# Attention of a macaron block: half slots of two key blocks replaced by groups of three, with one exponential a block

## The reference

```python
x = x + 0.5 * ffn(layernorm(x))
x = x + attn(layernorm(x))
x = x + 0.5 * ffn(layernorm(x))

def attn(x, WQ, WK, WV, WO):
    Q, K, V = (einsum('bsd,hkd->bhsk', x, W) for W in (WQ, WK, WV))
    scores = einsum('bhqd,bhkd->bhqk', Q, K) / sqrt(16)
    scores = where(tril(ones((4096, 4096))), scores, -inf)
    attn = einsum('bhqk,bhkv->bhqv', softmax(scores), V)
    return einsum('bhsv,hdv->bsd', attn, WO)
```

## Time and profile before

| | us |
|---|---|
| median of three runs | 1996.3 (1994.75 to 1996.97) |
| span of the profiled execution | 1995.0 |
| before attention's slots | 373.9 |
| attention with all three steps, 373.9 to 1728.8 | 1354.9 |
| the last 23 slots, without maxima | 51.9 |
| output projection and second feed-forward layer | 214.3 |

### The profile page before, as it was taken

The page is one execution under the profiler, slowest core; times in us unless marked ns, Lnnn a source line. Parts: engine busy times, 40 slices in busy tenths (PEclk is TensorE's granted clock), DMA queues, the critical chain, the costliest instruction groups (busy, mean ns, idle before and its releaser), DMA issues.

```text
span 1995.0 us, 58983 instructions
## 1 busy us (share of the span) xinstructions
PE 1949.6 (98%) x24312; PEld 1198.9 (60%) x24312; DVE 1677.5 (84%) x3630; ACT 1355.3 (68%) x1626; POOL 304.6 (15%) x736
## 2 busy tenths in 40 slices
PE   5999999999999999999999999999999999999999
PEld 3777776555555555555555555555555555569998
DVE  7655566699999999999999999999999999847663
ACT  5312221588888888888888888888888888884444
POOL 2100000011101111111110111111111101134444
PEclk9999999899999999999999999999999999999999
DMA  6111221212111111211111111111122111101110
GB/s 196 51 51 51 74 77 51 74 40 52 40 47 46 44 42 39 53 40 49 45 44 39 44 48 41 50 43 44 41 46 46 39 53 29 60 28 64 59 48 22
DMA packets 82812, 102.20 MB, mean 51 GB/s; under 512 B 16752, under 2 KB 45168, under 8 KB 82544
## 3 DMA queue, kind: packets, MB, share of 16 engines
q1 hardware_dynamic: 81920, 98.03, 17.4%
q10 hardware_dynamic: 624, 0.40, 0.1%
HBM read 68.46 MB, written 29.36 MB: 49 GB/s over the span
## 4 chain that ended last, share of the span: by engine, by line
PE 92%; DVE 4%; ACT 2%; issue 1%; DMA 1%; POOL 0%; SPq 0%; POOLq 0%; ACTq 0%; DVEq 0%
PE PS L1142 33%; PE PS L1269 32%; PE PS L1119 7%; PE PS L1089 6%; PE PS L1249 6%; PE PS L1328 4%; PE PS L1194 2%; PE PS L1113 1%; PE PS L1055 1%; ACT PG L700 1%; DVE BNS L745 1%; DVE OA L798 1%; DMA PG<-w_exp_t 1%; ACT OA L608 1%; POOL QT L577 0%
## 5 line engine op out<-in xcount | busy, mean ns | idle before, releaser
L700 ACT ACTIVATE PG<-PS 128x1024 f32<-128x1024 f32 (+1 forms) x1152 | 1116.0, 977 | 233.8 <-PE PS L1249 173.2
L930 DVE TENSOR_REDUCE MXP<-PS 128x1 f32<-128x512 f32 x1792 | 1099.7, 685 | 20.5 <-PE PS L1142 20.4
L1249 PE MATMUL PS<-QT,KT 50*128 50x512 f32 (+1 forms) x2304 | 802.3, 434 | 0.0
L1142 PE MATMUL PS<-KT,QT 48*128 48x512 f32 (+3 forms) x2304 | 797.1, 431 | 2.6 <-DVE MXP L930 2.3
L1269 PE MATMUL PS<-PG,VH 128*17 128x128 f32 x16896 | 727.5, 276 | 0.4 <-ACT PG L700 0.3
L1269 PEld LDWEIGHTS PS<-PG,VH 128*17 128x17 f32 x16896 | 400.5, 97 | 412.4 <-issue 363.4
L1142 PEld LDWEIGHTS PS<-KT,QT 48*128 48x128 f32 x2304 | 340.2, 185 | 251.8 <-issue 141.9
L1249 PEld LDWEIGHTS PS<-QT,KT 50*128 50x128 f32 x2304 | 335.1, 185 | 10.3 <-issue 9.9
L926 DVE CUSTOM_DVE_ANT_0 PS<-PS,MASK 128x128 f32<-128x128 f32 (+3 forms) x512 | 249.2, 506 | 72.7 <-PE PS L1142 66.9
L557 POOL TENSOR_SCALAR_AFFINE_SELECT PG<-PG 128x128 f32<-128x128 f32 x512 | 136.3, 292 | 995.8 <-ACT PG L700 995.0
L626 ACT ACTIVATE PG<-PS,GB 128x512 f32<-128x512 f32 x128 | 90.3, 706 | 171.3 <-PE PS L1089 171.3
(11 more groups left out here) (110 smaller groups left out, 1197.2 us busy)
## 6 DMA issues: line engine op xcount, KB each, us to landing
QT<-q_parts SPq DMA_DIRECT2D x256, 64.0 KB
KT<-k_parts SPq DMA_DIRECT2D x256, 64.0 KB
q_parts<-OA SPq DMA_DIRECT2D x16, 512.0 KB, 2.8
QT<-q_parts SPq DMA_DIRECT2D x256, 32.0 KB
k_parts<-OA SPq DMA_DIRECT2D x16, 512.0 KB, 4.6
KT<-k_parts SPq DMA_DIRECT2D x256, 32.0 KB
o_parts<-OS SPq DMA_DIRECT2D x128, 64.0 KB
OA<-o_parts SPq DMA_DIRECT2D x32, 256.0 KB
```

The costliest lines, as they stand in the source:

```text
L700: nc.scalar.activation(PB[n % 2][half][:, :, q0:TILE], PS[:, half * 1024:half * 1024 + 1024].rearrange("p (k q) -> p k q", k=2)[:, :, q0:T ...
L930: nc.vector.tensor_reduce(dst, bank(b), AX.X, ALU.max).then_inc(mx_red, 1)
L1142: mm(bank(4 + qs % 2 if b is None else b, w), q[0:SC, (BT * place(j) + qs) * P:(BT * place(j) + qs + 1) * P].bitcast(f32r), k[0:SC, c * TI ...
L1249: last = mm(PS[:, (2 * half + k) * 512 + q0:(2 * half + k + 1) * 512], kt[0:SM, kb * P:(kb + 1) * P].bitcast(f32r), qt[0:SM, place(j) * TI ...
```

## The change

The unit of work is the block, not the half slot. PE's loop takes groups of three units: score, maximum, score, maximum, score, maximum, and then three blocks of values, those of the group before (`VALUES_IN`; where a query tile ends within the three, the rest goes to the next group). Scores have three banks (0 to 2), one a unit; bank 3 goes to the maxima, which so have four. Each exponential takes one block of 512 columns (fewer on the diagonal: 512, 384, 256, 128, before 512, 512, 256, 256) into one of eight buffers. Semaphores count units. DVE's split steps start with the group after the last maximum of the half, one step behind each of three maxima and the fourth in the next group, and SP's `load_m` follows two slots after that. ACT waits, ahead of the first exponential, for the last stores of the parts of Q and K, since buffers for copied maxima are laid over them; a set `COPIED` of maxima that ACT would copy and POOL fold is there but empty, so none of this code runs. All other stages stay as they are.

```diff
+UNITS = [(j, c, k) for j, c in CH for k in range(BT)]
+GROUP = 3
+VALUES_BEHIND = 3
+S_BANKS = 3
+P_BUFFERS = 8
+COPIED = frozenset(())
-MAX_BANKS = (4, 5, 7)
+MAX_BANKS = (4, 5, 7, 3)
...
-        PB = [[PG[:, 4 * i + 2 * k:4 * i + 2 * k + 2, :] for k in range(2)] for i in range(2)]
+        PB = [PG[:, i, :] for i in range(P_BUFFERS)]
...
+        for g in range(GROUP_N):
+            last = min(GROUP * (g + 1) - VALUES_BEHIND, UNIT_N) if g < GROUP_N - 1 else UNIT_N
+            stop = next((u + 1 for u in range(first, last) if ends_tile(u)), last)
+            VALUES_IN.append(range(first, stop))
+            first = stop
...
+        def split_group(i):
+            return split_items(i)[-1] // GROUP + 1
...
+            def split_slot(i):
+                return (split_group(i) + 2) * GROUP // BT
...
-                    sp.wait_ge(st_ps[1], h * NCH + n + 1)
+                    sp.wait_ge(st_ps, (h * NCH + n + 1) * BT)
...
+            for w in range(1, 4):
+                act.wait_ge(parts_out[w], 16 * (NT + 1))
+
+            def exponential(u):
+                _, _, j, c, k = unit(u)
+                q0 = P * k if j == c else 0
+                if u >= P_BUFFERS:
+                    act.wait_ge(pv_done, u - P_BUFFERS + 1)
+                act.wait_ge(st_ps, u + 1)
+                nc.scalar.activation(PB[u % P_BUFFERS][:, q0:TILE], bank(u % S_BANKS)[:, q0:TILE],
+                                     ACT.Exp, scale=1.0 / DH ** 0.5).then_inc(exp_done, 1)
...
+            for g in range(GROUP_N):
+                for u in finals_in(g):
+                    final_maximum(u)
+                steps = splits_in(g)
+                for u in group_units(g):
+                    if u < MX_UNITS and not copied(u):
+                        _, n, _, _, qs = unit(max_item(u))
+                        maximum(max_item(u), n, qs, mx_bank(u))
+                    for i, k in steps[u % GROUP:u % GROUP + 1]:
+                        split_step(*divmod(i, 2), k)
...
+            def bank_free(u):
+
+                before = u - len(MAX_BANKS)
...
+                elif before >= 0:
+                    pe.wait_ge(mx_red, RED_N[before])
...
+            def scores(u):
...
+                if u >= S_BANKS:
+                    pe.wait_ge(exp_done, u - S_BANKS + 1)
+                kb = c * BT + k
+                kt, qt = (NK, NQ) if alone and u % 2 else (CK, CQ)
+                mm(bank(u % S_BANKS)[:, q0:TILE], kt[0:SM, kb * P:(kb + 1) * P].bitcast(f32r),
+                   qt[0:SM, place(j) * TILE + q0:(place(j) + 1) * TILE].bitcast(f32r),
+                   start=True, stop=True).then_inc(st_ps, 1)
...
-            for n in range(SLOT_N):
-                ahead_maximum(n, 0)
-                if n < H * NCH:
-                    scores(*divmod(n, NCH), 0)
...
-                ahead_maximum(n, 1)
-                if n:
-                    values(*divmod(n - 1, NCH), 0)
...
+            for g in range(GROUP_N):
+                for u in group_units(g):
+                    scores(u)
+                    ahead_maximum(u)
+                if g == 1:
+                    pe.wait_ge(att_init, 2)
+                for u in VALUES_IN[g]:
+                    values(u)
```

## The result

| | before | after |
|---|---|---|
| median, us | 1996.5 | 2010.2 (2005.3 to 2012.7) |
| ratio | | 1.0065, 95% interval 1.0049 to 1.0080 |
| span of the profiled execution | 1995.0 | 2003.5 |
| predicted | | 1950 (1915 to 1990) |

What follows compares the result with a forecast made beforehand. PE sets the pace now, DVE right behind and next to bound. A head falls from 88.0 to 84.7 us (83.0, 0.9, 0.8), 51 us in all; 1995.0 - 51 + 3 + 1.5 = 1948.5, so 1950 us (1915 to 1990).

Steps and rivals of the forecast that it cites:

- PE's group: PE in attention's steady part: three pairs and three blocks of values take 1.67 us, 80.2 us a head.
- DVE: Between diagonals DVE becomes the bound: three full maxima 1.80 us against PE's 1.67; floor 83.0 us a head.
- a burst of three does not starve DVE: Steady part: PE needs 1.7 us from a group's third maximum through the next first; four banks give DVE 2.4.
- ACT: Exponentials of 512 columns take 0.50 us each, three 1.50; by the skill page about 0.52, three 1.56.
- The loop over three score banks: Scores waiting for exponentials to free three banks: at least 1.73 us a group, under 1.80.
- What is moved on SP: `load_m` two slots later lands 1.7 us too late at each head's first score; 0.9 paid, bounds 0 and 4.6.
- DVE's store of 0.8 us: At a head's first score DVE has some 0.8 us stored, so 0.9 of PE's 1.7 us wait is paid.
- The clock: Rival: PE's granted clock falls after each head's starting wait, giving back 46 us, about 1995 us; chance 0.04.
- one of the signs of a wrong forecast: In attention: a group of 1.83 or more with DVE idle, ACT without idle time, or the granted clock falling.
- The start: ACT's first exponential waits for the last stores of Q and K parts, landed by 379.4: +3 us (0 to 6).
- The tail: Last 92 blocks, without maxima: ACT at 1.50 us for three, plus copies of sums; +1.5 us (-1 to +9).
- the rival on ACT: 512-column exponentials do not overlap (0.597): 1.83 us a group, 88.4 a head, 2015 us in all; chance 0.10.

Runs made afterwards that it cites:

- groups of two: Changed kernel with split maxima issued two slots earlier, but groups of two key blocks and values two blocks behind: 2011.2 us, ratio 1.0085.
- the early load: Changed kernel with the four DMAs of the split maxima put back two slots earlier in SP's order, as before: 1947.4 us, ratio 0.9750.
- the kernel before with the late load: Kernel before the change, with only the split-maxima DMAs two slots later in SP's order: 2059.2 us, ratio 1.0315.
- the run that gave it: Changed kernel with nine extra 512-column matmuls before PE's wait for the split maxima at heads 1 to 15: 1988.3 us, ratio 0.9953.

## Why the prediction was wrong, point by point

**PE's group: right.** Forecast 1.67; where nothing holds PE up, starts are 1.67 to 1.68 apart (1089.10 to 1092.45 is two groups), and the 24 value records begin 0.78 before the next pair. The groups of two give 88.0 a head and those of three 84.1, which is the gain claimed for fewer changes between pairs and values, as far as DVE lets it through.

**DVE: right.** Without the price of `load_m` the forecast was 83.0 + 0.8 = 83.8 us a head; the early load has 84.07, with DVE busy 98.2%. That a burst of three does not starve DVE holds with four banks and only with four.

**ACT: right.** 0.48 us an exponential for the 0.50 forecast. The 0.52 that the prediction's estimate gave by the Trainium skill's page "ScalarE: Activation LUTs", section "What ACT_TABLE_LOAD costs", is not borne out by the 15 exponentials in the row above. The loop over three score banks, forecast at 1.73 a group, is seen in the tail, at 1.61 and 1.76 in turn.

**What is moved on SP: wrong, the step that decided.** Its distances were right. SP passed its wait 4.6 us before the head could have begun (forecast 4.9: the groups there take 1.67, not 1.80), and from there to the landing the sum was 2.4 + 2.6 + 1.6 = 6.6. SP's order of time ahead of head 8 in the changed kernel, which answers to the earlier trace rows:

```profile
1082.58 0.60 SPq L462 DMA_DIRECT2D QT<-q_parts  x1
...
1083.75 0.60 SPq L455 DMA_DIRECT2D KT<-k_parts  x1
...
1084.85 2.63 SPq L474 DMA_DIRECT2D QT<-MT  x4
```

and the chain that ended last from the issue of the fourth transfer on (start us, us, what):

```profile
1086.88 1.98 DMA QT<-MT
1088.85 0.25 issue
1089.10 0.47 PE PS L1348
```

1082.58 to 1089.10 is 6.5. So the wait was forecast at 1.7 and is 2.3 on the mean (34.8 / 15). What failed is what I made of it. I let DVE's store of 0.8 us pay for half; DVE at the same place shows that it had no such store:

```profile
1082.68 0.70 DVE L1014 CUSTOM_DVE_ANT_0 PS<-PS,MASK 128x512 f32<-128x512 f32 x1 [0.17 <-PE PS L1238]
...
1084.34 0.57 DVE L1014 CUSTOM_DVE_ANT_0 PS<-PS,MASK 128x384 f32<-128x384 f32 x1 [0.28 <-PE PS L1238]
...
1085.47 2.48 DVE L1018 TENSOR_REDUCE MXP<-PS 128x1 f32<-128x512 f32 x4
1089.64 0.69 DVE L1018 TENSOR_REDUCE MXP<-PS 128x1 f32<-128x512 f32 x1 [1.69 <-PE PS L1238]
```

The diagonal slots just before the head have emptied it (0.17 and 0.28 us of waiting for PE), so of PE's 1.96 us DVE loses 1.69: a store of some 0.3 us in place of 0.8. Where the clock stays up behind a head's start and the next head waits 2.35 or 2.62, the head takes 86.2 or 86.5, 2.2 or 2.4 over the 84.07: the wait is paid nearly whole. The 0.9 a head should have been 2.2.

**The clock: the rival that came, with a chance of 0.04.** I had its mechanism and its sign; I set it aside since the trace of before showed a clock of 1.00 through 1215 us of changes between pairs and values. But in those PE never waited. Nor does show a long wait: PE was idle for 0.24 of the 3.20 us ahead of it (374.3 to 377.5). A row that bears on it, and that I did not weigh, stands a little earlier in the trace of before, where PE waits 2.28 us for DVE and then runs at the lower level (it had been busy for 1.52 of the 4.00 us up to 362.0):

```profile
362.01 1.10 PE L1142 MATMUL PS<-KT,QT 48*128 48x512 f32 x2 [2.28 <-DVE MXP L930]
...
363.20:366.50 3.30, 3.30 (x8) 2.57 (x9) 1.48 (x6) 0.52 (x1) 0.00 (x0) 0.50 0.00 0
```

Both rows spoke for the rival, and I weighed them by the many that were further off. A clock that falls inside attention is also one of the signs of a wrong forecast that the prediction names. The size was nearer: 3.1 us a head forecast, at least 1.4 net (21 over 15 heads); four waits leave the clock alone. The 0.9 that I charged for `load_m` became 4.0 with the clock (59.4 / 15). The Trainium skill's page "TensorE: Matmul & The Clock Gate" describes, in the section "HAM oscillation — how this bites in real kernels", a kernel in which PE is throttled anew at each wait for a DMA; it lies nearer to this case than the section on psum queues which the prediction weighed, though its kernel waits after every short piece of work. The traces agree in part: the clock fell at 11 of 15 waits of 1.00 to 2.87 us, at all 15 of 2.68 to 4.71, and in the kernel before with the late load at 7 of 14 of 0.75 to 2.13.

**The start: too small.** Forecast +3 (0 to 6); the wait costs 8.2 us in all (the first head with it and without), from which goes what the kernel before lost there already (3.1 by the earlier trace rows): 5.1. The forecast counted blocks and left the clock out: in the first head it is at the lower level for 10.2 us with the wait, for 6.8 in the kernel before, and not at all without the wait. The stores were taken to land by 379.4; the last landed some 1.7 us later, as the first exponential at 381.12 shows.

**The tail: too small.** Forecast +1.5 (-1 to +9) with 1.50 a group. The loop that the prediction had worked out for the middle, at 1.73, holds there too (1.61 and 1.76 in turn), and I did not carry it over: the 92 blocks took 56.1 us in place of 51.9, +4.2, and the fourth score bank gives 5.0 of the tail back (3.2 to 4.4 of the whole time).

**The sum.** With `load_m` early: 15.36 heads of 88.0 - 84.07 are 60.4, less 5.1 and 4.2, 51.1; the spans say 49.1 (1995.0 to 1945.9), and in the second trace attention begins 2.0 us later (375.9 against 373.9). The early load's 1947.4 lies by the forecast of 1950 only because errors cancel: 14 us charged for `load_m` (0.9 x 15), against 5 too few at start and tail and 4 in the heads. Put `load_m` where the change has it, and 57.6 go: 1945.9 + 57.6 = 2003.5. Two figures of the prediction do not follow from its own sums, and neither bears on the miss: the low end of 1915 (1950 less 1.7 x 15.36 is 1924) and the 88.4 of the rival on ACT (48 groups of 1.83 are 87.8).

What stays open: why the clock stayed up behind four waits, one of them (2.37 us) longer than some that brought it down, and fell in other runs behind waits of 0.83 and 0.11. The executions of one kernel differ in this, as the scatter of the run without the store wait shows. And of the 59.4 us the parts of wait and clock are known only to some 10 us: 21 is the least for the clock, since three falls are left in the run that gave it.

## What to carry to other kernels

When a step moves to a later slot of a queue, compare its landing with the first instruction that needs it, and if it is late, charge the wait whole unless the trace shows, at that very place, that the bound engine has work stored. A wait of TensorE of one or two microseconds in an otherwise unbroken stretch is priced with the clock that may fall behind it; look for the places in the trace where PE did wait, however short. And a larger burst on one engine may need more buffers towards the engine that it feeds: here groups of three paid only together with the fourth bank.

## What the runs showed of the hardware that was not expected

- Single short waits of PE in unbroken work brought the granted clock to the lower level: in the changed kernel 11 of 15, all of 2.2 to 2.9 us, for 3.4, 6.8 or 10.2 us; in the kernel before with the late load 7 of 14, of 0.83 to 2.13 us, for 3.4 to 13.7 us and once for 37.5. The length alone does not decide: waits of 2.37 and 1.42 us in the same two runs, and one of 0.4 us with the load one slot earlier, did not, and with extra matmuls ahead of the wait it fell once behind 0.11 us.
- The price of such a fall is not fixed from one execution to the next: the changed kernel without the store wait gave 1986 to 2012 us, at mean granted clocks of 0.988 and 0.970, where the one with the early load stays between 1944.9 and 1948.2.
- Nine matmuls of no use ahead of the waits made the kernel 22 us faster; the clock fell at three heads in place of eleven.
